# A three-layer decoder kernel: the last batches' sums and bases stay on chip, two of them are gated by VectorE, and the orders of issue are rewritten

## The reference, cut to what matters

```python
x = x + attn(layernorm(x))                    # self attention, 16 heads, + bff
x = x + xattn(ctx, ctx, layernorm(x))         # one head over 750 context rows, + bo
h = layernorm(x)
scores = (h q_w^T r_w^T)(keys r_w^T)^T / sqrt(48) + mask      # 224 x 2048 a batch
w = softmax(top8(scores)); agg = sum_k w_k * aux_values[idx_k]
u = clip(0.5 * log1p(var(h)) / mean_over_all(log1p(var(h))) + 2.5 * sigmoid(learned(h)), 0, 5)
out = x + (h + sigmoid(gate_w1 * u + gate_bias) * agg)
```

## Time and profile before

| what | value |
|---|---|
| device time, median of 3 (range) | 2828.26 us (2824.99 to 2828.69) |
| profiled execution: its own time | 2849.81 us |
| its span | 2847.7 us |
| PE busy | 2571.2 us (90%) |
| DVE busy | 2142.2 us (75%) |
| ACT busy | 1443.6 us (51%) |
| POOL busy | 694.1 us (24%) |
| mean DMA rate | 127 GB/s |

### The profile page before, as it was taken

The page is one execution under the profiler, slowest core; times in us unless marked ns, Lnnn a source line. Parts: engine busy times, 40 slices in busy tenths (PEclk is TensorE's granted clock), DMA queues, the critical chain, the costliest instruction groups (busy, mean ns, idle before and its releaser), DMA issues. The chain is left out here.

```text
span 2847.7 us, 56945 instructions
## 1 busy us (share of the span) xinstructions
PE 2571.2 (90%) x19090; PEld 2098.2 (74%) x19090; DVE 2142.2 (75%) x4203; ACT 1443.6 (51%) x4252; POOL 694.1 (24%) x652
## 2 busy tenths in 40 slices
PE   6699999999999999999999999999999999999720
PEld 3477788877887888778887888778787888778510
DVE  4446788888888888888887888888888888787641
ACT  2345545555555555555555555555555455555252
POOL 0000222222222222222222222222222222222344
PEclk8799999999999999999999999999999999999855
DMA  5212444444444444444444445444444444444888
GB/s 185 52 52 69 127 108 137 127 135 116 127 126 126 130 104 141 122 130 121 132 117 129 126 113 135 129 128 122 132 114 129 116 127 133 131 112 114 226 198 170
DMA packets 132519, 360.72 MB, mean 127 GB/s; under 512 B 21986, under 2 KB 26594, under 8 KB 124243
## 3 DMA queue, kind: packets, MB, share of 16 engines
q1 hardware_dynamic: 68468, 198.53, 24.0%
q0 software_dynamic: 64000, 161.52, 22.8%
HBM read 316.83 MB, written 43.15 MB: 126 GB/s over the span
## 5 line engine op out<-in xcount | busy, mean ns | idle before, releaser
L589 POOL DMA_INDIRECT vg<-in_L_ffn_aux_values,idx x512 | 501.9, 980 | 858.1 <-DVE agg L999 627.8
L660 ACT ACTIVATE pa<-psA,nmax 112x224 f32<-112x224 f32 x1024 | 443.7, 449 | 263.2 <-DVE nmax L891 152.5
L891 DVE TENSOR_REDUCE nmax<-psA 112x4 f32<-112x896 f32 x256 | 267.4, 1086 | 139.8 <-PE psA L1170 139.8
L1104 PE MATMUL psX<-big,gT 128*112 128x375 f32 x1024 | 333.4, 478 | 0.6 <-ACT gT L687 0.6
L999 DVE SCALAR_TENSOR_TENSOR agg<-vg,wt,agg 112x512 f32<-112x512 f32 x420 | 314.6, 749 | 9.6
L1104 PE MATMUL psX<-pT,cx 125*128 125x224 f32 x1536 | 299.1, 355 | 0.0
L1104 PEld LDWEIGHTS psX<-pT,cx 125*128 125x128 f32 x1536 | 288.0, 190 | 4.0 <-issue 0.3
L906 DVE TENSOR_TENSOR pa<-pa,rsum 112x896 f32<-112x896 f32 x256 | 279.6, 1092 | 8.9 <-DVE rsum L904 0.2
L1113 PE MATMUL psA<-ident,pa 112*112 112x112 f32 x2048 | 238.3, 265 | 42.5 <-DVE oT_lo L869 23.0
L1104 PEld LDWEIGHTS psX<-big,gT 128*112 128x112 f32 x1024 | 175.5, 176 | 125.7 <-issue 0.9
L1113 PEld LDWEIGHTS psA<-ident,pa 112*112 112x112 f32 x2048 | 202.3, 135 | 78.9 <-DVE pa L906 33.7
(11 more groups left out here) (217 smaller groups left out, 6033.5 us busy)
## 6 DMA issues: line engine op xcount, KB each, us to landing
big<-in_ctx_t SPq DMA_DIRECT2D x32, 1500.0 KB, 8.3
cx<-in_ctx SPq DMA_DIRECT2D x32, 1344.0 KB
xa<-in_x SPq DMA_DIRECT2D x64, 224.0 KB, 2.9
centered<-in_x_t SPq DMA_DIRECT2D x32, 448.0 KB
x<-in_x SPq DMA_DIRECT2D x32, 448.0 KB, 4.2
x<-in_L_attn_bff POOLq DMA_DIRECT2D x32, 448.0 KB
x<-cb_scratch POOLq DMA_DIRECT2D x32, 448.0 KB, 6.0
out<-x SPq DMA_DIRECT2D x32, 448.0 KB, 3.1
```

Of the source, the lines that this page charges most:

```text
L589: pool.indirect_dma_start(vg[:, c % SLOTS, k, :], None, aux_values, bass.IndirectOffsetOnAxis(ap=idx[:, t, n:n + 1], axis=0))\
L660: last = nc.scalar.activation(pa[:, t, h, :], psA[0:R, h, t * S:(t + 1) * S], ACT.Exp, bias=nmax[:, k % 2, h, t:t + 1], accum_out=rsum[:, ...
L891: nc.vector.tensor_reduce(nmax[:, k % 2, h:h + 2, :], psA[0:R, h:h + 2, 0:T * S].rearrange("p h (t s) -> p h t s", t=T), AX_X, ALU.max, ne ...
L1104: last = nc.tensor.matmul(dst, stationary, moving, start=n == 0, stop=n == len(pairs) - 1)
```

## The change

Seven edits go together:

1. `DIRECT` becomes 29: the sums of batches 29, 30 and 31 stay on chip (29 in a tile laid over `qkT`). There are then 29 loads instead of 30, and no tile is used twice.
2. The bases of batches 30 and 31 are no longer stored when they are ready. The base of 30 is written to a tile laid over `xT`, that of 31 stays in `x2`. X out of batch 31 waits for the base of 30 instead of its store.
3. Batches 30 and 31 are gated by DVE: `merge` computes sum * gate + base in two instructions and SP stores the result plainly, in place of ACT's scale and POOL's accumulating DMA.
4. In `ORDER`, R bias moves behind F top 1 and A mix 3, to the end of the iteration. R load moves ahead of G sum 7.
5. In `ORDER`, X prob 1 moves ahead of G sum 4, F score 0 and A mix 1; G sum 6 moves ahead of X mix 0.
6. In `ORDER`, X norm / A value, F norm / X query and N spread / G sum 2 swap places.
7. `LAST` is rewritten, the loads as well as the sums and scales.

```diff
 ORDER = (
     ("A", "qk", 0), ("A", "qk", 1), ("A", "score", 0), ("G", "sum", 0), ("A", "share", 0), ("X", "enter", 0),
-    ("A", "value", 0), ("X", "norm", 0), ("G", "sum", 1), ("A", "qk", 2), ("X", "turn", 0), ("A", "prob", 0),
-    ("X", "query", 0), ("F", "norm", 0), ("A", "score", 1), ("N", "norm", 0), ("F", "turn", 0), ("X", "score", 0),
-    ("G", "sum", 2), ("N", "spread", 0), ("G", "sum", 3), ("A", "qk", 3), ("A", "share", 1), ("X", "score", 1),
+    ("X", "norm", 0), ("A", "value", 0), ("G", "sum", 1), ("A", "qk", 2), ("X", "turn", 0), ("A", "prob", 0),
+    ("F", "norm", 0), ("X", "query", 0), ("A", "score", 1), ("N", "norm", 0), ("F", "turn", 0), ("X", "score", 0),
+    ("N", "spread", 0), ("G", "sum", 2), ("G", "sum", 3), ("A", "qk", 3), ("A", "share", 1), ("X", "score", 1),
     ("N", "center", 0), ("F", "route", 0), ("A", "mix", 0), ("X", "prob", 0), ("A", "prob", 1), ("F", "learn", 0),
-    ("G", "sum", 4), ("F", "score", 0), ("A", "mix", 1), ("X", "prob", 1), ("F", "score", 1), ("G", "sum", 5),
-    ("A", "score", 2), ("F", "top", 0), ("A", "share", 2), ("X", "mix", 0), ("G", "sum", 6), ("X", "mix", 1),
+    ("X", "prob", 1), ("G", "sum", 4), ("F", "score", 0), ("A", "mix", 1), ("F", "score", 1), ("G", "sum", 5),
+    ("A", "score", 2), ("F", "top", 0), ("A", "share", 2), ("G", "sum", 6), ("X", "mix", 0), ("X", "mix", 1),
     ("A", "prob", 2), ("F", "score", 2), ("A", "score", 3), ("X", "out", 0), ("A", "share", 3), ("X", "out", 1),
-    ("A", "mix", 2), ("A", "prob", 3), ("G", "sum", 7), ("R", "load", 0), ("F", "score", 3), ("R", "bias", 0),
-    ("F", "top", 1), ("A", "mix", 3),
+    ("A", "mix", 2), ("A", "prob", 3), ("R", "load", 0), ("G", "sum", 7), ("F", "score", 3), ("F", "top", 1),
+    ("A", "mix", 3), ("R", "bias", 0),
 )
...
+    ("Z", "load", 14, 31), ("X", "enter", 0, 31), ("G", "sum", 0, 29), ("Z", "load", 11, 31), ("X", "norm", 0, 31),
...
+    ("Z", "load", 5, 31), ("Z", "log", 0, 31), ("Z", "gate", 0, 31), ("Z", "load", 13, 31), ("G", "sum", 2, 30),
+    ("Z", "scale", 0, 31), ("Z", "scale", 1, 31), ("G", "sum", 3, 30), ("Z", "scale", 2, 31), ("F", "turn", 0, 31),
+    ("F", "route", 0, 31), ("G", "sum", 4, 30), ("Z", "load", 25, 31), ("Z", "scale", 3, 31), ("Z", "scale", 4, 31),
+    ("Z", "scale", 5, 31), ("F", "learn", 0, 31), ("G", "sum", 5, 30), ("Z", "scale", 6, 31), ("Z", "gate", 1, 31),
+    ("F", "score", 0, 31), ("F", "score", 1, 31), ("F", "top", 0, 31), ("Z", "load", 28, 31), ("Z", "scale", 7, 31),
...
+    ("Z", "scale", 10, 31), ("G", "sum", 7, 30), ("F", "score", 3, 31), ("F", "top", 1, 31), ("Z", "scale", 11, 31),
+    ("Z", "load", 20, 31), ("Z", "scale", 12, 31), ("Z", "scale", 13, 31), ("Z", "scale", 14, 31),
+    ("G", "sum", 0, 31), ("G", "sum", 1, 31), ("Z", "scale", 15, 31), ("G", "sum", 2, 31), ("Z", "scale", 16, 31),
+    ("G", "sum", 3, 31), ("G", "sum", 4, 31), ("Z", "scale", 17, 31), ("Z", "scale", 18, 31),
+    ("Z", "scale", 19, 31), ("G", "sum", 5, 31), ("Z", "scale", 20, 31), ("Z", "load", 24, 31),
...
+    ("Z", "scale", 27, 31), ("Z", "scale", 28, 31), ("Z", "scale", 29, 31), ("G", "sum", 7, 31),
+    ("Z", "scale", 30, 31), ("Z", "scale", 31, 31),
 )
...
+        base30 = nc.alloc_sbuf_tensor_at("over_xT", [R, T, D], F32, offset=xT_at)
...
-        DIRECT = B - 2
+        DIRECT, WHOLE = B - 3, B - 2
+        base = {WHOLE: base30, WHOLE + 1: x2}
...
+            def store_whole(_, n):
+                if n >= WHOLE:
+                    sp.wait_ge(merged, n - WHOLE + 1)
+                    sp.dma_start(tiles(row(out, n)), late_tile[n]).then_inc(late_stored[LATE + n - DIRECT], 16)
+
             def store_base(b, _):
+                if isinstance(b, int) and b >= WHOLE:
+                    return
...
             def add_base(b, _):
                 pool.wait_ge(x2_normed, b + 1)
-                nc.gpsimd.tensor_tensor(x2[:, :, :], x2[:, :, :], xnf[:, :, :], ALU.add).then_inc(base_ready, 1)
+                dst = x2
+                if isinstance(b, int) and b >= WHOLE:
+                    dst = base[b]
+                    wait_full(pool, "A", FILL["A", "mix", NB - 1], B - 1)
+                nc.gpsimd.tensor_tensor(dst[:, :, :], x2[:, :, :], xnf[:, :, :], ALU.add).then_inc(base_ready, 1)
...
+            def merge(_, n):
+                if n < WHOLE:
+                    return
+                dve.wait_ge(gate_ready, 1 + (n == B - 1))
+                dve.wait_ge(base_ready, n + 1)
+                dve.wait_ge(summed, CHUNKS * (n + 1))
+                for t in range(T):
+                    last = nc.vector.scalar_tensor_tensor(late_tile[n][:, t, :], late_tile[n][:, t, :], gate[:, T * n + t:T * n + t + 1],
+                                                          base[n][:, t, :], ALU.mult, ALU.add)
+                last.then_inc(merged, 1)
```

In the new `LAST` SP has only its loads before the two stores of the merged batches: the stores of base 30 and 31 and of the sums of batch 29 are gone from it. The old one, in its second half:

```diff
-    ("X", "out", 0, 31), ("X", "out", 1, 31), ("G", "sum", 1, 30), ("F", "norm", 0, 31), ("Z", "log", 0, 31),
-    ("Z", "load", 21, 31), ("Z", "gate", 0, 31), ("Z", "scale", 0, 31), ("G", "sum", 2, 30), ("Z", "scale", 1, 31),
-    ("Z", "scale", 2, 31), ("Z", "scale", 3, 31), ("Z", "scale", 4, 31), ("Z", "load", 15, 31),
-    ("F", "turn", 0, 31), ("Z", "scale", 5, 31), ("Z", "scale", 6, 31), ("F", "route", 0, 31),
-    ("Z", "load", 19, 31), ("F", "learn", 0, 31), ("Z", "load", 25, 31), ("G", "sum", 3, 30), ("F", "score", 0, 31),
-    ("G", "sum", 4, 30), ("Z", "load", 27, 31), ("Z", "scale", 7, 31), ("G", "sum", 5, 30), ("F", "score", 1, 31),
-    ("F", "top", 0, 31), ("Z", "scale", 8, 31), ("Z", "load", 28, 31), ("G", "sum", 6, 30), ("Z", "scale", 9, 31),
...
-    ("G", "sum", 2, 31), ("Z", "scale", 15, 31), ("G", "sum", 3, 31), ("G", "sum", 4, 31), ("Z", "scale", 16, 31),
-    ("Z", "scale", 17, 31), ("Z", "scale", 18, 31), ("G", "sum", 5, 31), ("G", "sum", 6, 31),
-    ("Z", "scale", 19, 31), ("Z", "scale", 20, 31), ("Z", "load", 26, 31), ("Z", "scale", 21, 31),
```

More of the change, by code:

```diff
@@ L173, in build @@
         centered = sb("centered", [P, C, S])
+        xT_at = (nc.sbuf_base + 31) // 32 * 32
         xT = (sb("xT_hi", [P, C, S], F32R), sb("xT_lo", [P, C, S], F32R))
+        base30 = nc.alloc_sbuf_tensor_at("over_xT", [R, T, D], F32, offset=xT_at)
+        qk_at = (nc.sbuf_base + 31) // 32 * 32
         qkT = (sb("qk_hi", [P, 2, 2 * S], F32R), sb("qk_lo", [P, 2, 2 * S], F32R))
+        over_qk = nc.alloc_sbuf_tensor_at("over_qk", [R, T * D], F32, offset=qk_at)
         va = sb("va", [R, T, H, DH])
@@ L393, in build @@
         LATE = len(late)
-        DIRECT = B - 2
+        DIRECT, WHOLE = B - 3, B - 2
+        base = {WHOLE: base30, WHOLE + 1: x2}
         GATED = (slice(0, T * (B - 1)), slice(T * (B - 1), T * B))
-        kept = [pa[:, :, :, :].rearrange("p t h s -> p (t h s)"), paT[:, :, :, :].rearrange("p t h s -> p (t h s)")]
+        kept = [over_qk[:, :], pa[:, :, :, :].rearrange("p t h s -> p (t h s)"), paT[:, :, :, :].rearrange("p t h s -> p (t h s)")]
         late_tile = [late[n % LATE] for n in range(DIRECT)] + [rows_of(w) for w in kept]
         late_loaded = [sem(f"late_loaded{k}") for k in range(LATE)]
-        late_stored = [sem(f"late_stored{k}") for k in range(LATE + 2)]
-        scaled = sem("scaled")
+        late_stored = [sem(f"late_stored{k}") for k in range(LATE + B - DIRECT)]
+        scaled, merged = sem("scaled"), sem("merged")
         block = stack.enter_context(nc.Block())
@@ L540, in load_agg @@
                 sp.dma_start(late[k], tiles(row(agg_dram, n))).then_inc(late_loaded[k], 16)
-            pipeline(sp, {("Z", "load"): load_agg, ("W", "split"): after_split, ("W", "keys"): after_keys,
+            pipeline(sp, {("Z", "load"): load_agg, ("Z", "scale"): store_whole, ("W", "split"): after_split, ("W", "keys"): after_keys,
                           ("W", "cb"): first_cxT, ("W", "gb"): first_ctx,
@@ L547, in _ @@
                           ("G", "sum"): store_agg})
-            for k in range(LATE + 2):
-                sp.wait_ge(late_stored[k], 16 * (1 + (k < DIRECT - LATE)))
+            for k in range(LATE + B - DIRECT):
+                if k < DIRECT or k >= LATE:
+                    sp.wait_ge(late_stored[k], 16 * (1 + (k < DIRECT - LATE)))
         @block.gpsimd
@@ L770, in scale @@
                     act.wait_ge(summed, CHUNKS * (n + 1))
-                act.wait_ge(gate_ready, 1 + (n == B - 1))
+                act.wait_ge(gate_ready, 1)
                 for t in range(T):
@@ L949, in x_out @@
                     dve.wait_ge(x1_biased, 16 * (b + 1))
-                    wait(dve, base_stored, 16 * b)
+                    if isinstance(b, int) and b == B - 1:
+                        dve.wait_ge(base_ready, b)
+                    else:
+                        wait(dve, base_stored, 16 * b)
                 j = FILL["X", "out", t]
@@ L1084, in gates @@
                 nc.vector.tensor_scalar(cols, cols, 0.0, 5.0, ALU.max, ALU.min).then_inc(clip_ready, 1)
-            pipeline(dve, {("Z", "log"): log_sum, ("Z", "gate"): gates,
+            def merge(_, n):
```

(5 more changed lines are left out.)

## The result

| | before | after |
|---|---|---|
| device time, median (range) | 2826.62 us (2824.95 to 2828.69) | 2804.8 us (2800.8 to 2806.97, 4 runs) |
| profiled execution: own time, span | 2849.81, 2847.7 | 2803.22, 2801.2 |

The ratio is 0.9921, with a 95% interval of 0.9904 to 0.9938: 22 us faster, where 2 us slower (2830) was forecast. Every ratio here is to the kernel before, timed beside that run; its median moved between 2825.66 and 2826.91 us.

What follows compares the result with a forecast made beforehand. The prediction took PE, with DVE's chain level, to bound the loop and the DMA engines the end, except in holes. Loop +20, earlier X prob 1 and G sum 6 0, last stage -18: +2 on 2828.3, 2830 us; range 2808 to 2848.

Steps and rivals of the forecast that it cites:

- No slack worth counting: Loop, at X turn: DVE's chain is level with PE; PE waited 0.23 us and started 0.13 us after DVE's X norm.
- part 1: Loop: four gathers answer F top 1's search, R bias lands 11.5 us after it, X enter 0.7 us later: +20 us.
- The earlier R load costs nothing and brings nothing: Loop, R load ahead of G sum 7: effect zero, because the bias no longer waits for it.
- Size of the chain: Loop, search end to bias landing: 0.8 + 4.6 + 0.15 + 5.9, together 11.5 us; bounds +3 and +53 us.
- Part 2: Loop, X prob 1 and G sum 6 earlier: 0, bounds -3 and +5 us.
- Part 3: Last stage, all its terms together: -18 us, bounds -26 and -2.
- Start: Last stage: X enter of batch 31 comes 3.3 us later, gates +3 us, bounds +1 and +6.
- Loads: Last stage: late loads no longer held by base 31's store go earlier, -10 us, bounds -14 and -4.
- Holes: Last stage: fewer accumulates between gathers close 10 of 14 us of DMA holes, -10 us, bounds -14 and 0.
- Accumulates against plain stores: Last stage: two accumulates fewer, -4.6 us, two plain stores on q1 instead, +3.5 us.
- Merges: Last stage: four DVE instructions, 3.1 us, then SP's stores, hidden by ten queued accumulates (23 us): 0.
- A: Rival: bias stays hidden, landing by 1522.0; loop -3, end -18, so 2807 us; chance 0.17.

Runs made afterwards that it cites:

- a0: The kernel before, unchanged, profiled once more: median of 12 runs 2826.59 us, ratio 1.000; this profiled execution took 2822.46 us.
- e1: The kernel before with edit 4 alone (R bias to the end of the iteration, R load ahead of G sum 7): 2820.16 us, ratio 0.9979.
- e4: The kernel before with the whole new `ORDER` and the old `LAST`, sums, bases and scales: 2820.5 us, ratio 0.998.
- e2: The kernel before with edit 4, the first two chunks' gathers made to wait for the search of tile 1: 2893.41 us, ratio 1.0232.
- e3: The kernel before with edit 5 alone (X prob 1 and G sum 6 earlier): 2828.6 us, ratio 1.0006.
- t1: The changed kernel with the old `ORDER`, so edits 1, 2, 3 and 7 only: 2809.93 us, ratio 0.9945.
- t4: The changed kernel with SP's load 25 and the nine behind it waiting until POOL has added base 31: 2807.82 us, ratio 0.9932.
- t2: The changed kernel with the old `LAST`, less the load of batch 29: 2817.63 us, ratio 0.9971.
- t5: The changed kernel with SP alone on the new `LAST`, all other engines on the old one without load 29: 2812.14 us, ratio 0.9955.
- t6: The changed kernel with SP alone on the old `LAST` without load 29, all other engines on the new one: 2801.61 us, ratio 0.9913.
- t3: The changed kernel with edits 2 and 3 undone (bases stored, nothing merged), in the new `LAST`: 2812.75 us, ratio 0.9951.
- b1: The changed kernel with X enter and X norm moved ahead, A share 0 and G sum 0 behind A value: 2984.44 us, ratio 1.056.

## Why the prediction was wrong, point by point

- **What bounds the kernel: right for the end, wrong in one claim for the loop.** "No slack worth counting" rested on a profiled execution 21.6 us above the median. In a0 DVE had about 1.2 us of slack a turn there, and PE's wait for `nx` is 1.4 us in 1700. Why that first execution ran 80.4 us a turn is open: in it DVE waited 83.3 us for PE's scores ahead of its maxima, against 52.6 in a0, at the same granted clock of 1.00.
- **The failed step: part 1, "Worked from the search's end".** The four gathers were taken to answer the search of F top 1. They belong to the first tile, whose search is long done, and what releases them is a slot. That the gathers stood behind the bias, which went just as the search ended, was read as a wait for the search; it showed POOL's own order. The prediction had the row that tells it, the bias's 24.48 us of waiting for the load of x, and did not ask what stood behind it. The whole +20 us went with that step; -6 (e1, e4) stands in its place, a difference of 26 us where the whole forecast missed by 24. e2 puts the assumed wait in and gets +67.
- **"The earlier R load costs nothing and brings nothing": not tested alone.** The bias waited for that load 684 us over 29 turns in a0 and 4.9 us in the changed kernel, but e1 moves load and bias together. A bias issued as late as a0's (1497.62, landing 5.9 us later at 1503.5) would still land 5 us before a0's X enter (1508.55), so an estimate from a0's rows gives the load's place little to bring.
- **Size of the chain, had it existed:** 12.6 us instead of 11.5, the landing 6.8 instead of 5.9. With e2's +67 that is beyond the far bound of +53. "No gather follows it closely" overlooked the four ahead of it in the same queue.
- **The Trainium skill's price** (page "DMA: Bandwidth & Descriptors", section "Anatomy of one DMA"), an estimate of 3.1 us for this DMA: no run agrees, with 5.8 us in the changed kernel and 6.8 in e2.
- **Part 2: right.** e3 measured +2.5 us with an interval that holds zero; 0 was forecast.
- **Part 3: right in sum, -18 against -17 (t1), the terms less so.** Start: +3 forecast for the gates, +3.9 measured: from PE's first product of batch 31's projection to the end of the first gate on DVE it is 2690.69 - 2609.05 = 81.6 us against 77.8 in a0. The first accumulate comes 86.1 us after that product against 80.3, +5.8, since two gathers now stand ahead of it in POOL's stream. Loads: -10 forecast, and all were issued before the first accumulate, as forecast; but -4 measured for the first hold beside the new mix (t4), and both holds with the accumulates only -3 beside the old one (t2 less e4). Holes: -10 forecast, with -12 in the stages and -8 to -15 for the mix (t5 and t6): the larger term. Accumulates against plain stores: -1.1 forecast; in the new list -8 with edits 2 and 3 (t3), of which about 4 are t4's late loads, as base 31 is stored again ahead of them. By itself the term wasn't measured. Merges: 0, right. That the sum came out within 1 us of t1 is partly luck, since loads were too large and holes too small.
- **The rivals.** A gave 2807 and is the outcome, but its ground (a bias landing by 1522.0 on a short chain) was not what happened. It had 0.17. Its case for the loop, -3, was closest of all. The range began at 2808 and so left A's own figure out.

## What to carry to other kernels

Before a step on an in-order queue is said to wait for an event, read the count in its wait and work out to which item it belongs; two rows 0.3 us apart show the queue's order and not a release. A long wait on such a queue is paid by what stands behind it. A step moved in a shared list moves on every engine that has a part in it: b1 lost the cover that PE's part gave. Where one profile lies 0.8% off the median, take no claim of slack from it. In a tail that is bound by a queue, count its empty time stage by stage: the mix that keeps an in-order engine from blocking the work that feeds the queue was worth more here than earlier loads.

## What the runs showed that was not expected

- The same 448 KB accumulating DMA lands 5.8 us after its issue with two gathers just ahead of it (changed kernel) and 6.8 us with four (e2).
- In b1 the granted clock falls after PE has stood still for 4.66 us. It was 1.00 (2.4 GHz) before that wait and 0.50 (1.2 GHz) for 6.2 us after it:

```profile
1506.00:1513.40 7.40, 7.40 (x45) 1.00 0.39 62
1518.80:1525.00 6.20, 6.12 (x29) 0.50 0.21 36
1525.00:1570.00 45.00, 44.49 (x328) 1.00 0.38 114
```

  These rows are PE's alone (us, busy time, clock, DMA share, GB/s). The first product of A value took 0.53 us there against 0.28 in the changed kernel. A turn is 5.7 us longer than the changed kernel's, of which 4.66 - 1.43 = 3.2 us are waiting. The other 2.5 us are about what the slow stretch costs: an estimate from its row is 3 us, half of 6.12. In the changed kernel PE's longest wait in the loop was 1.4 us and the clock stayed at 1.00.
